# A vision-transformer kernel with its feed-forward, triangular solve and second attention in one unrolled phase, and the images solved in two groups

## The chip, the cores and the metric

The kernel runs on one core of one Trainium2 chip. The metric is the device time of one execution in microseconds (us), median over several runs. TensorE (PE) multiplies matrices into PSUM, VectorE (DVE), ScalarE (ACT) and GpSimd (POOL) work elementwise, and SyncE (SP) issues most transfers. GpSimd does not touch PSUM here. Engines run their own instruction streams in order and meet at semaphores.

## The reference, cut to what matters

64 images of 96x96 become 37 tokens of 256 features each. Then come: a first attention (16 query heads, one key/value head), a gated feed-forward whose gates are an entmax over 16 experts, a second attention that is a delta rule inside one chunk per image, and a mixture of 8 experts with one expert per token. The change lies in the feed-forward and the second attention, which for each image and each of two heads of 128 features is:

```python
k = x / max(norm(x), 1e-12)                    # x: the layernormed tokens, one head
beta = sigmoid(x @ W_beta.T); v = (x @ W_write.T) * beta; k_beta = k * beta
A0 = tril(-(k_beta @ k.T) * L, -1)             # L: decay by distance
A = solve_triangular(eye - A0, eye, lower=True, unit_diagonal=True)
v = A @ v                                      # state is zero: one chunk only
o = tril((k @ k.T) * L) @ v
h = h + layernorm(h) + o @ W_read.T            # roughly: the layer adds its own input
```

The solve is therefore 128 systems (64 images by 2 heads) of size 37x37.

## The kernel before, in words

Everything is fp32. 2368 token rows lie in SBUF as 22 tiles of 111 rows (3 images), worked on as 11 pairs of tiles. A phase is a block of the five engines' streams, ended by a barrier that also clears the phase's semaphores. The phases are:

1. Embedding and first attention, unrolled by hand. SyncE loads the first image tile, then the embedding weights (`in_params`), then the second tile; ScalarE's queue loads the identity and the other first weights, and, once `in_params` is there, 4.1 MB of later weights (lines 311 to 313 and 608 to 612). TensorE's first instruction waits for `in_params`.
2. Gates for all tiles at once, mostly on VectorE.
3. Feed-forward and keys (from line 880), a loop over pairs (`run_turns`, a hardware loop with a software pipeline three pairs deep). Per pair TensorE does `first_products`, `hidden` (eight chunks, through Gelu on ScalarE in `activate`), `second_products` (line 955), `outputs`, and, two turns later for each tile j, `turn_rows_and_keys` (line 979) and `row_products` (989, 995). VectorE does `gate_first`, `gate_second` (1092, each after a copy of the gate out of PSUM), `add_outputs` (1101), `normalise` (241 to 253), `key_squares`, `key_inverses` (1131, 1134) and `decay_products` (1141 to 1146). GpSimd does `prepare_keys` (250, 1175 to 1179). The normalised keys are a second set of rows, so a tile is transposed in four pieces: two of rows, two of keys.
4. The solve (from line 1184), for all 128 systems at once, one on each partition. VectorE scales the matrices by beta, SyncE stores them to `n_rows` in DRAM (line 1220) and loads them back with one system on a partition (1224), VectorE does the forward substitution (lines 1266 and 1272: one multiply and one reduce per row i = 1..36, in two column parts from i = 8 on, so that less is multiplied by zero), and SyncE stores the inverses to `a_rows` (1231). Behind the loads SyncE starts the 12.6 MB of expert weights that fit by now (1226, 1228).
5. Second attention (from line 1282), again `run_turns`. SyncE loads each tile's inverses (1304). Per tile: `spread_inverses` on GpSimd (1332), `solve_values` (1364), `attend` (1375), `read_out` (1386), `turn_rows` (1397) and `router_logits` (1407) on TensorE, copies on ScalarE, `add_and_norm` (1483, 241 to 253) and `keep_logits` (1495) on VectorE, and a store of the finished rows to `x_rows` (1311).
6. Routing (VectorE) and, at the end, 26 tiles of 128 gathered tokens through the experts (from line 1640). The change does not touch these.

Of the kernel before, what the change touches and what calls it, by code (L numbers as in the profile page):

```python
# [9 lines left out]

# [5 lines left out]
ALU = mybir.AluOpType  # L16
# [27 lines left out]
RL = 112  # L44
ROW_CUTS = ((0, 96), (96, R))
# [23 lines left out]
def build(nc, x_h, pack1_h, pack2_h, packc_h, w1_h, w2_h, out_h):  # L69
# [9 lines left out]
    with ExitStack() as top:  # L79
# [58 lines left out]
        beta_img = carve_1(NT * H1 * IPT, R)  # L138
        carve_1b = carver(arena_w2, W2S // 2)
        gate_t = carver(arena_w2, W2S // 2 + NT * H1 * R)(NT * R, E0)  # L140
# [3 lines left out]

        in_params = sem("in_params")
# [112 lines left out]
        with phase():  # L258
# [49 lines left out]
            @block.sync  # L308
            def _(sp):
                embed_w = at1["w_q"][0]  # L310
                sp.dma_start(xp[0], x_h[0]).then_inc(x_in[0], 16)
                sp.dma_start(pack1[:, 0:embed_w], pack1_h[:, 0:embed_w]).then_inc(in_params, 16)
                sp.dma_start(xp[1], x_h[1]).then_inc(x_in[1], 16)
                for i in range(1, PAIRS):
                    for j in range(2):
                        sp.wait_ge(embedded[j], i)
                        sp.dma_start(xp[j], x_h[2 * i + j]).then_inc(x_in[j], 16)

            @block.tensor
            def _(pe):  # L320
                pe.wait_ge(in_params, 16)
# [7 lines left out]
                def embed(i, j):  # L329
# [4 lines left out]
                    for k in range(PC):  # L334
                        mm = nc.tensor.matmul(bank[0][0:R, j * D:(j + 1) * D], xp[j][:, k * R:(k + 1) * R], w_lin[:, k, :],  # L335
# [270 lines left out]
            def _(act):  # L606
                embed_w = at1["w_q"][0]
                act.dma_start(ident, packc_h[:, 0:128]).then_inc(in_ident, 16)
                act.dma_start(pack1[:, embed_w:], pack1_h[:, embed_w:]).then_inc(in_qkv, 16)
                act.wait_ge(in_params, 16)  # L610
                for part, source, arrived in ((pack2, pack2_h, in_params2), (cst[:, 128:], packc_h[:, 128:], in_cst)):
                    act.dma_start(part, source).then_inc(arrived, 16)
                act.wait_ge(in_qkv, 16)
# [128 lines left out]
        with phase():  # L742
# [15 lines left out]
            beta = ec(NT * H1, R)  # L758
            nk = ec(NT * H1 * TOK, R)
# [112 lines left out]
        with phase():  # L872
            (z1_done, g1_out, z1_gated, hid_done, hid_act, z2_done, g2_out, z2_gated, y_done, y_added) = (
                psem(n) for n in ("z1_done", "g1_out", "z1_gated", "hid_done", "hid_act", "z2_done", "g2_out", "z2_gated",
                                  "y_done", "y_added"))
            stats = [pair("st"), pair("ag"), pair("ve")]
            (powered, normed, sq_done, roots, rooted, floored, inverted, k_ready, turned, t_ready, v_done, g_done,
             v_out, n_masked, n_reduced) = (
                pair(n) for n in ("powered", "normed", "sq_done", "roots", "rooted", "floored", "inverted", "k_ready",
                                  "turned", "t_ready", "v_done", "g_done", "v_out", "n_masked", "n_reduced"))  # L880
            rows_free = pair("rows_free")
            W = 2 * R
            bc = carver(arena_w1, n1w + n2w + 2 * H1 * R + 2 * H1 + NT * H1 * (TOK + 1))
            z1, z2, g1, g2 = (bc(W) for _ in range(4))
            hid = bc(OC * W)
            wc = carver(work)
            xn = [wc(D, R) for _ in range(2)]
            st = [wc(8, R) for _ in range(2)]
            ve = [wc(4, R) for _ in range(2)]
            cc = carver(arena_w1)  # L890
            kn = [cc(D, R) for _ in range(2)]
            xk = [cc(4 * R) for _ in range(2)]
            sq = [cc(D, R) for _ in range(2)]
            nf = [cc(H1 * R, R) for _ in range(2)]
            sc = [cc(12, R) for _ in range(2)]
            block = enter(nc.Block())


            HB = OC // 2
# [3 lines left out]

# [1009 lines left out]
```

## Time and profile before

| | |
|---|---|
| median of 3 runs | 863.99 us (863.92 to 864.47) |
| profiled execution | 865.1 us, of which the span on the page is 863.3 us |
| PE busy, share of span | 678.2 us (79%) |
| DVE busy | 455.9 us (53%) |
| ACT, POOL busy | 237.3 us (27%), 246.7 us (29%) |
| mean granted TensorE clock | 0.884 of full speed |

A share is a mean over phases that are bound by different engines, so the stages have to be read one by one. The profiled execution is 1.1 us above the median of the runs. Busy time of TensorE is modelled at its ends, and a matmul of fp32 shows as several records.

### The profile page before, as it was taken

What the parts mean: (1) busy time and instruction counts of PE and PEld (TensorE: products, weight loads), DVE (VectorE), ACT (ScalarE), POOL (GpSimd) and SP (SyncE); (2) the same over time, 40 slices, a digit from 0 to 9 for tenths busy, and PEclk for the clock granted to TensorE, in tenths of its full rate; (3) what the DMA queues carried; (4) which work ended last, traced back from release to release, by engine and by line L of the source; (5) the groups of instructions that cost most, each with busy time, mean ns of one, the idle gap of its engine ahead of it and who ended that gap; (6) DMA issues with size and microseconds to landing.
All of it is one profiled execution on the core that took longest, in us unless ns stands there. A gap on an engine that the chain in (4) does not pass through costs nothing. (4 is left out here: it accounts for less than half of the span.)

```text
span 863.3 us, 14177 instructions
## 1 busy us (share of the span) xinstructions
PE 678.2 (79%) x4606; PEld 513.0 (59%) x4606; DVE 455.9 (53%) x1216; ACT 237.3 (27%) x615; POOL 246.7 (29%) x330
## 2 busy tenths in 40 slices
PE   4799999999976079999994000899269999999995
PEld 2567777777754058888873000688156766776673
DVE  1457777777764826666765197366623333333331
ACT  0223333333321143424333000355103223323321
POOL 1344444444441003343342000233011122222211
PEclk9899999999986569999997555799659999999998
DMA  8111111111000000000000993322510111111110
GB/s 339 44 34 33 33 34 33 33 34 33 1 2 1 0 2 0 1 0 0 0 0 0 118 438 127 68 84 84 226 49 25 49 56 49 45 55 55 44 37 18
DMA packets 21542, 49.31 MB, mean 57 GB/s; under 512 B 12451, under 2 KB 12581, under 8 KB 20719
## 3 DMA queue, kind: packets, MB, share of 16 engines
q1 hardware_dynamic: 17583, 33.21, 12.8%
q0 software_dynamic: 3328, 10.23, 3.8%
q10 hardware_dynamic: 576, 5.15, 1.5%
q8 instruction: 33, 0.54, 0.2%
q14 instruction: 22, 0.18, 0.1%
HBM read 38.72 MB, written 9.86 MB: 56 GB/s over the span
## 5 line engine op out<-in xcount | busy, mean ns | idle before, releaser
L1707 PE MATMUL psum<-arena_w,work 128*128 x208 | 95.5, 603 | 1.0 <-DVE work L1759 1.0
L1805 ACT ACTIVATE work<-psum,cst 128x128 f32<-128x128 f32 x208 | 56.7, 383 | 144.0 <-PE psum L1720 143.9
L1731 PE MATMUL psum<-arena_w,work 128*128 x416 | 94.2, 379 | 0.4 <-ACT work L1805 0.4
L1731 PEld LDWEIGHTS psum<-arena_w,work 128*128 128x128 f32 x416 | 77.1, 190 | 10.5 <-issue 1.1
L1364 PE MATMUL psum<-tokens,work 111*111 (+1 forms) x88 | 16.1, 310 | 72.7 <-POOL work L1332 71.8
L1768 DVE COPY work<-psum 128x512 f32<-128x512 f32 x52 | 35.9, 691 | 69.8 <-PE psum L1707 69.8
L1669 POOL DMA_INDIRECT out<-work,row_i x26 | 25.7, 988 | 159.9 <-DVE work L1781 159.9
L335 PE MATMUL psum<-arena_w 128*111 128x256 f32 x264 | 64.2, 396 | 8.9 <-DMA arena_w<-in_pack 8.9
L1707 PEld LDWEIGHTS psum<-arena_w,work 128*128 128x128 f32 x208 | 38.2, 194 | 39.8 <-issue 39.8
L335 PEld LDWEIGHTS psum<-arena_w 128*111 128x111 f32 x264 | 46.8, 183 | 23.5 <-DMA arena_w<-in_pack 8.9
L704 POOL TENSOR_TENSOR arena_w<-arena_w,work 101x592 f32<-101x592 f32 x33 | 39.5, 1197 | 71.8 <-DVE work L566 71.8
L250 POOL TENSOR_TENSOR work<-work 111x1 f32<-111x1 f32 x44 | 24.4, 555 | 119.3 <-DVE work L246 119.3
L1364 PEld LDWEIGHTS psum<-tokens,work 111*111 111x111 f32 x88 | 12.0, 193 | 73.7 <-POOL work L1332 71.9
L695 POOL TENSOR_TENSOR arena_w<-arena_w 128x296 f32<-128x296 f32 x66 | 43.8, 685 | 22.3 <-DVE arena_w L534 22.3
L1775 DVE TENSOR_TENSOR tokens<-psum,cst 128x256 f32<-128x256 f32 x26 | 11.0, 424 | 73.6 <-PE psum L1731 73.6
L389 PE MATMUL psum<-arena_w 128*37 128x296 f32 x264 | 41.5, 436 | 3.3 <-ACT arena_w L658 3.3
L941 PE MATMUL psum<-arena_w 128*128 128x222 f32 x176 | 39.8, 372 | 1.7 <-DVE arena_w L1081 1.0
L627 ACT COPY arena_w<-psum 37x592 f32<-37x592 f32 x33 | 25.2, 765 | 57.7 <-PE psum L400 57.7
L546 DVE TENSOR_REDUCE work<-psum 101x16 f32<-101x592 f32 x33 | 25.4, 771 | 24.2 <-PE psum L389 24.2
L253 DVE TENSOR_SCALAR work<-tokens,work 111x256 f32 (+1 forms) x44 | 22.5, 512 | 29.5 <-POOL work L250 29.5
L941 PEld LDWEIGHTS psum<-arena_w 128*128 128x128 f32 x176 | 33.1, 198 | 7.3 <-issue 3.0
L955 PE MATMUL psum<-arena_w 128*128 128x222 f32 x176 | 36.2, 357 | 0.0
(214 smaller groups left out, 1332.8 us busy)
## 6 DMA issues: line engine op xcount, KB each, us to landing
arena_w<-in_w SPq DMA_DIRECT2D x2, 4096.0 KB, 13.8
arena_w<-in_x SPq DMA_DIRECT2D x22, 333.0 KB, 2.9
x_rows<-tokens SPq DMA_DIRECT2D x22, 192.0 KB, 2.0
arena_w<-in_pack ACTq DMA_DIRECT2D x1, 2420.0 KB, 8.5
cst<-in_packc ACTq DMA_DIRECT2D x1, 1727.0 KB, 13.1
arena_w<-in_pack SPq DMA_DIRECT2D x1, 1024.0 KB, 7.6
arena_w<-in_pack ACTq DMA_DIRECT2D x1, 818.5 KB, 8.1
work<-a_rows SPq DMA_DIRECT2D x22, 32.4 KB, 2.0
```

What stands on the lines that cost most here:

```text
L335: mm = nc.tensor.matmul(bank[0][0:R, j * D:(j + 1) * D], xp[j][:, k * R:(k + 1) * R], w_lin[:, k, :], start=(k == 0), stop=(k == PC - 1))
L389: mm = nc.tensor.matmul(bank[4 + f][e * HP:e * HP + TOK, 0:HH * TOK], qt[:, a:a + TOK], kb[p % 2 * 2 + e], start=True, stop=True)
L695: nc.gpsimd.tensor_tensor(kb[p % 2 * 2 + e].rearrange("p (h s) -> p h s", h=HH), kt[:, a:a + TOK].unsqueeze(1).broadcast_to([128, HH, TOK] ...
L704: nc.gpsimd.tensor_tensor(by_head(prob[p % 2], HP), by_head(prob[p % 2], HP), small[p % 2][:, 2 * NH:3 * NH].unsqueeze(2).broadcast_to([PR ...
L941: mm = nc.tensor.matmul(bank[2 + f // 2 % 2][:, (f % 2) * W:(f % 2 + 1) * W], w_out1[:, f, :], z1, start=True, stop=True)
L955: mm = nc.tensor.matmul(bank[1][:, W:2 * W], w_in2[:, f, :], hid[:, f * W:(f + 1) * W], start=(f == 0), stop=(f == OC - 1))
L1364: mm = nc.tensor.matmul(bank[j][0:R, h * 128:(h + 1) * 128], ab[j][:, h * R:(h + 1) * R], tokens[0:R, bass.ds((2 * i + j) * RW + D + h * 1 ...
L1669: pool.indirect_dma_start(out_h, bass.IndirectOffsetOnAxis(ap=row_i[:, 2 * i + j:2 * i + j + 1], axis=0), yo[j], None).then_inc(y_stored[j ...
L1707: mm = nc.tensor.matmul(bank[2 * j + f][:, :], xgt[j][:, k * 128:(k + 1) * 128], arena_w1[:, bass.ds(expert * (2 * FF) + (k * FF + f * 512 ...
L1731: mm = nc.tensor.matmul(bank[7][:, 0:D], ht[j][:, g * 128:(g + 1) * 128], arena_w2[:, bass.ds(expert * (FC * D) + g * D, D)], start=(g == ...
L1768: nc.vector.tensor_copy(hp[j][:, f * 512:(f + 1) * 512], bank[2 * j + f][:, :]).then_inc(h_out[j], 1)
L1805: nc.scalar.activation(ht[j][:, g * 128:(g + 1) * 128], bank[4 + f][:, k * 128:(k + 1) * 128], ACT.Gelu, bias=cst[:, bass.ds(expert * FC + ...
```

## The change

- The first transfers all go through SyncE's queue, in order of need, with the embedding weights in two halves; TensorE waits only for the half that it is about to use. The 4.1 MB of later weights start after the first attention's weights are there.
- Phases 3, 4 and 5 become one phase, unrolled in Python, without barriers in between.
- Keys are no longer normalised rows. The inverse norm of a head (`inv_all`) is folded into `beta`, into the strength that scales the system matrix, and into `add_read`. ScalarE makes the squares with a running sum (`squares`), beta comes from a Tanh in place of a Sigmoid over all tiles at the end, and GpSimd makes the small factors (`inverses`, `strengths`), which VectorE's scaling of the system matrices uses at once. Transposes per pair fall from 8 to 4.
- The two gate products are copied out of PSUM by ScalarE in one piece (`copy_gates`), not by VectorE in two. The reduction of the masked products over the three images is two adds on GpSimd (`fold`), and each tile's systems are stored as soon as they are made.
- The images are solved in two groups: pairs 0 to 5 (36 images, 72 systems) and pairs 6 to 10 (28 images, 56 systems). In the second group each system lies on two partitions, with every other column on each. VectorE takes the substitution in pieces between its other work: `SLOTS` gives the budget of each piece.
- SyncE's order: systems of group 0 stored, then loaded; systems of group 1 stored; inverses of group 0 stored; systems of group 1 loaded; inverses of group 0 loaded; 8.4 MB of expert weights; inverses of group 1 stored and loaded; 4.2 MB of expert weights; all finished rows.

The diff, cut to its core:

```diff
+GROUPS = ((0, 6), (6, PAIRS))
+SLOTS = (1.0, 1.0, 5.0, 1.7)
...
-                sp.dma_start(pack1[:, 0:embed_w], pack1_h[:, 0:embed_w]).then_inc(in_params, 16)
+                for k in range(2):
+                    part = slice(k * w_lin_w // 2, (k + 1) * w_lin_w // 2)
+                    sp.dma_start(pack1[:, part], pack1_h[:, part]).then_inc(in_embed[k], 16)
                 sp.dma_start(xp[1], x_h[1]).then_inc(x_in[1], 16)
+                sp.dma_start(pack1[:, w_lin_w:embed_w], pack1_h[:, w_lin_w:embed_w]).then_inc(in_params, 16)
+                sp.dma_start(ident, packc_h[:, 0:128]).then_inc(in_ident, 16)
+                sp.dma_start(pack1[:, embed_w:], pack1_h[:, embed_w:]).then_inc(in_qkv, 16)
...
-                pe.wait_ge(in_params, 16)
...
+                        if i == j == 0 and k % 3 == 0:
+                            pe.wait_ge(in_embed[k // 3], 16)
...
+                def load_systems(g):
+                    im0, im1, nb, stride, sets = group_of(g)
...
+                        sp.wait_ge(n_stored[b], 16 * len(ROW_CUTS) * len(range(b, stored, NB)))
...
+                for g in range(len(GROUPS)):
+                    for t in range(2 * GROUPS[g][0], 2 * GROUPS[g][1]):
+                        store_systems(t)
+                    if g:
+                        store_inverses(g - 1)
+                    load_systems(g)
+                for g in range(LAST):
+                    load_inverses(g)
...
+                sp.dma_start(arena_w1[:, :], w1_h).then_inc(w1_in, 16)
+                store_inverses(LAST)
+                load_inverses(LAST)
+                sp.dma_start(arena_w2[:, 0:W2S // 2], w2_h[:, 0:W2S // 2]).then_inc(w2a_in, 16)
+                for t in range(NT):
+                    sp.wait_ge(normed2, t + 1)
...
+                for i in range(-1, PAIRS + 2):
+                    second_products(i - 1)
+                    first_products(i)
+                    row_products(i - 2, 0)
+                    outputs(i - 1)
+                    hidden(i, range(OC // 2))
+                    row_products(i - 2, 1)
+                    gates(i + 1)
+                    hidden(i, range(OC // 2, OC))
+                    turn_rows(i - 1)
...
+                for t in range(NT + 3):
+                    solve_values(t)
+                    read_out(t - 1)
+                    turn_outputs(t - 3)
+                    attend(t)
+                    router_logits(t - 3)
...
+                    for k in range(2 * H1):
+                        a = 2 * H1 * i + k
+                        last = nc.scalar.activation(junk[:, k * 128:(k + 1) * 128], xn[i % 2][:, k * 128:(k + 1) * 128], ACT.Square,
+                                                    accum_out=ss[:, a:a + 1])
...
+                    nc.scalar.activation(th[:, t * H1:(t + 1) * H1], bank[6][0:R, D:D + H1], ACT.Tanh,
+                                         scale=0.5).then_inc(beta_out, 1)
+                    nc.scalar.copy(x_half(t), bank[6][0:R, 0:D]).then_inc(v_out, 1)
...
+                for i in range(-1, PAIRS + 2):
+                    copy_rows(i - 2)
+                    keep_values(i - 2, 0)
+                    activate(i, range(HB // 2))
+                    keep_values(i - 2, 1)
+                    copy_gates(i + 1)
+                    activate(i, range(HB // 2, HB))
+                    squares(i - 1)
...
+                    nc.vector.tensor_tensor(attn_t[:, t * H1 * R:(t + 1) * H1 * R], bank[7][0:R, 0:H1 * R], lt, ALU.mult)
+                    dve.wait_ge(strong, t + 1)
+                    free(dve, nk_ready, t - 1)
+                    for h in range(H1):
+                        cols = slice(h * R, (h + 1) * R)
+                        last = nc.vector.scalar_tensor_tensor(nf[t % 2][:, cols], bank[7][0:R, cols],
+                                                              strength[:, t * H1 + h:t * H1 + h + 1], ln[:, cols],
+                                                              ALU.mult, ALU.mult)
...
+                    nc.vector.memset(sys_x[:, 0:cols * TOK], 0.0).then_inc(zeroed[g], 1)
...
+                    dve.wait_ge(n_in[g], 16 * H1 * sets)
...
+                    yield 1.5
+                    last_cut = 0
+                    for i in range(1, TOK):
+                        cut = CUTS[i] // sets if CUTS[i] < i else i
...
+                            cost += 2 * (0.16 + (c1 - c0) * (end - j0) / 960)
...
+                def advance(budget):
+
+                    while pending[0] is not None and budget > 0:
+                        cost = next(pending[0], None)
+                        if cost is None:
+                            pending[0] = None
+                        else:
+                            budget -= cost
...
+                    for k, mark in enumerate((half_added, added)):
+                        nc.vector.scalar_tensor_tensor(h, bank[4 + j][0:R, k * D:(k + 1) * D],
+                                                       inv_all[:, t * H1 + k:t * H1 + k + 1], h,
+                                                       ALU.mult, ALU.add).then_inc(mark, 1)
...
+                for i in range(-1, PAIRS + 2):
+                    gate_second(i - 1)
+                    gate_first(i)
+                    advance(SLOTS[0])
+                    if i - 2 in ends:
+                        advance(math.inf)
+                    decay_products(i - 2, 0)
+                    add_outputs(i - 1)
+                    advance(SLOTS[1])
+                    normalise(i - 1)
+                    decay_products(i - 2, 1)
+                    if i - 2 not in ends:
+                        advance(SLOTS[2])
+                    elif ends[i - 2] < LAST:
+                        pending[0] = substitution(ends[i - 2])
+                advance(math.inf)
+                pending[0] = substitution(LAST)
+                firsts = [2 * p0 for p0, _ in GROUPS]
+                for t in range(NT + 3):
+                    if t == firsts[LAST]:
+                        advance(math.inf)
+                    normalise_outputs(t - 2)
+                    add_read(t - 1)
+                    keep_logits(t - 3)
+                    if t > 0:
+                        advance(SLOTS[3])
...
+                for i in range(-1, PAIRS + 2):
+                    strengths(i - 2, 0)
+                    fold(i - 2, 0)
+                    power_rows(i - 1)
+                    strengths(i - 2, 1)
+                    add_rows(i - 1)
+                    fold(i - 2, 1)
+                    inverses(i - 1)
+                for t in range(-1, NT + 1):
+                    power_outputs(t - 1)
+                    spread_inverses(t + 1)
```

## Rows read from the trace of the kernel before

**Rows 1.** The page's part 2: TensorE's busy tenths and granted clock in 40 slices.

```profile
PE   4799999999976079999994000899269999999995
...
PEclk9899999999986569999997555799659999999998
```

**Rows 2.** Stretches: length; busy PE, PEld, DVE, ACT, POOL; PE clock; DMA share; GB/s.

```profile
342.74:355.22 12.48, 12.48 (x70) 11.05 (x69) 8.36 (x25) 5.14 (x14) 4.72 (x8) 1.00 0.01 2
...
446.27:472.50 26.23, 15.37 (x69) 11.89 (x68) 14.35 (x41) 7.90 (x24) 9.02 (x14) 0.80 0.00 0
472.50:495.40 22.90, 0.00 (x0) 0.00 (x0) 3.50 (x6) 0.22 (x1) 0.41 (x1) 0.50 0.84 95
495.40:533.20 37.80, 0.00 (x0) 0.00 (x0) 36.74 (x130) 0.00 (x0) 0.00 (x0) 0.50 0.73 313
...
542.40:551.50 9.10, 8.07 (x32) 7.01 (x33) 1.99 (x6) 1.81 (x5) 2.68 (x5) 0.54 0.47 67
551.50:603.70 52.20, 50.57 (x345) 42.60 (x343) 34.46 (x115) 27.29 (x78) 19.99 (x37) 1.00 0.29 84
603.70:610.30 6.60, 4.02 (x24) 3.03 (x23) 3.03 (x13) 2.15 (x7) 1.10 (x2) 0.88 0.35 102
```

**Rows 3.** Timeline of TensorE in the feed-forward: start, duration, engine, line.

```profile
330.26 3.29 PE L955 MATMUL psum<-arena_w 128*128 128x222 f32 x16
...
338.92 0.35 PE L979 MATMUL psum<-cst,work 111*128 111x111 f32 x2
...
339.11 0.35 PE L979 MATMUL psum<-cst,arena_w 111*128 111x111 f32 x2
...
406.99 3.29 PE L955 MATMUL psum<-arena_w 128*128 128x222 f32 x16
```

**Rows 4.** Groups of instructions of VectorE and ScalarE by shape, 350 to 630 us.

```profile
L241 DVE BATCH_NORM_STATS2 work<-tokens 111x6 f32 x31 | 13.3, 428 | 4.6 <-issue 2.2
...
L1141 DVE TENSOR_TENSOR arena_w<-psum,arena_w 111x222 f32 x15 | 5.8, 390 | 0.0
L1101 DVE TENSOR_TENSOR tokens<-tokens,psum 111x512 f32 x8 | 5.4, 679 | 0.0
...
L1092 DVE SCALAR_TENSOR_TENSOR arena_w<-psum,arena_w 128x222 f32<-128x222 f32 x8 | 3.6, 451 | 0.3
...
L1065 ACT ACT_TABLE_LOAD x1 | 1.3, 1283 | 0.1
```

**Rows 5.** Timeline around the solve and into the second attention, all engines.

```profile
475.01 6.95 SPq L1220 DMA_DIRECT2D n_rows<-arena_w  x4
...
489.22 1.15 SPq L1224 DMA_DIRECT2D arena_w<-n_rows  x2
...
539.00 12.02 SPq L1304 DMA_DIRECT2D work<-a_rows  x22
...
542.36 1.08 POOL L1332 TENSOR_TENSOR work<-work,arena_w 111x222 f32<-111x222 f32 x2 [68.24 <-DMA work<-a_rows]
...
548.42 0.42 DVE L1483 TENSOR_TENSOR tokens<-tokens,psum 111x256 f32<-111x256 f32 x1 [9.25 <-PE psum L1386]
...
576.44 0.69 PE L1364 MATMUL psum<-tokens,work 111*111 x4
```

**Rows 6.** DMA issues of the page's part 6: KB each, median us to landing.

```profile
a_rows<-arena_w SPq DMA_DIRECT2D x2, 342.2 KB, 4.0
x_rows<-tokens SPq DMA_DIRECT2D x22, 30.0 KB, 2.0
```

**Rows 7.** The first transfers and matmuls: stretches of the span, then the timeline.

```profile
0.00:10.00 10.00, 1.14 (x3) 0.91 (x4) 1.46 (x5) 0.00 (x0) 2.85 (x9) 1.00 0.82 289
...
8.86 8.35 PE L335 MATMUL psum<-arena_w 128*111 128x256 f32 x24 [8.86 <-DMA arena_w<-in_pack]
```

**Rows 8.** Two lines of VectorE: duration in ns, least, median, most.

```profile
L253 DVE TENSOR_SCALAR work<-tokens,work x44: 412/414/644, 328.5 to 607.7; 111x256 f32 x32, 111x256 f32<-111x256 f32 x12
...
L1131 DVE TENSOR_SCALAR arena_w<-arena_w x22: 158/678/684, 330.9 to 465.3; 111x2 f32<-111x2 f32 x22
```

More of the change, by code:

```diff
@@ L872, in build @@
         with phase():
[L873 to L880, printed above, removed]
@@ new lines, in build @@
+            n_in, solved, a_stored, zeroed, diagonal = (
+                [psem(f"{name}{g}") for g in range(len(GROUPS))]
+                for name in ("n_in", "solved", "a_stored", "zeroed", "diagonal"))
+            chain = pair("chain")
+            a_in = [psem(f"a_in{t}") for t in range(NT)]
+            x_stored = psem("x_stored")
+            block = enter(nc.Block())
+            W = 2 * R
+            HB = OC // 2
+            LAST = len(GROUPS) - 1
+            fc = carver(arena_w1, n1w + n2w + 2 * H1 * R + 2 * H1)
@@ L1010, in _, with solve_values @@
-                run_turns(pe, turn, behind=2)
+                        key = xk[:, (2 * j + h) * R:(2 * j + h + 1) * R]
+                        mm = nc.tensor.matmul(bank[7][0:R, h * R:(h + 1) * R], key, key, start=True, stop=True)
+                    mm.then_inc(g_done, 1)
+                def solve_values(t):
+                    if not tile(t):
+                        return
+                    pe.wait_ge(a_block, t + 1)
+                    free(pe, vn_out, t - 1)
+                    for h in range(H1):
+                        mm = nc.tensor.matmul(bank[t % 2][0:R, h * 128:(h + 1) * 128], ab[t % 2][:, h * R:(h + 1) * R],
+                                              x_half(t)[:, h * 128:(h + 1) * 128], start=True, stop=True)
+                    mm.then_inc(vn_done, 1)
@@ new lines, in attend @@
+                def attend(t):
+                    if not tile(t):
+                        return
+                    pe.wait_ge(vn_out, t + 1)
+                    free(pe, o_out, t - 1)
+                    for h in range(H1):
+                        a = (t * H1 + h) * R
+                        mm = nc.tensor.matmul(bank[2 + t % 2][:, h * R:(h + 1) * R], vn[t % 2][:, h * 128:(h + 1) * 128],
+                                              attn_t[:, a:a + R], start=True, stop=True)
+                    mm.then_inc(o_done, 1)
@@ new lines, in router_logits @@
+                def router_logits(t):
+                    if not tile(t):
+                        return
+                    pe.wait_ge(xt_ready, t + 1)
+                    for k in range(2):
+                        mm = nc.tensor.matmul(bank[6 + t % 2][0:R, 2 * R:2 * R + NE], xt[t % 2][:, k * R:(k + 1) * R],
+                                              w_r[:, k, :], start=(k == 0), stop=(k == 1))
+                    mm.then_inc(logits, 1)
+                for i in range(-1, PAIRS + 2):
[8 more added lines that the diff above has]
+                    turn_rows(i - 1)
```

884 lines of the change are left out of this document (399 added, 485 removed).

## The prediction

> **What bounds the kernel now.** I read first TensorE's busy tenths and clock over the span [rows 1]. TensorE is full except in three places: a gap near 280 to 310 us (gates), one from about 455 to 545 us, and routing near 615 us. The change works on the second, and on the first microseconds.
>
> The busy times by stretch [rows 2] show what the second gap is made of. A steady turn of the feed-forward lasts 12.48 us with TensorE busy for all of it and VectorE for 8.36. From 446.27 the pipeline runs out for 26.2 us. Then 22.9 us pass with every engine nearly idle (systems to DRAM and back), 37.8 us with VectorE alone (the solve), and 9.2 us, up to the start of the row at 542.40, of storing and reloading inverses. TensorE does nothing for 69.9 us. In the second attention it is busy again for 50.57 of 52.2 us, so that stage is bound by TensorE at 2.7 us a tile.
>
> The largest possible gain is thus some 70 us. The question is how much of the solve finds room on VectorE. The mistake to avoid is to count it as hidden because two stages overlap: solving is VectorE's work, and VectorE has work of its own in both.
>
> **The start.** The first matmul starts at 8.86 us, when all 1 MB of embedding weights has landed, together with 1.2 MB of others; 289 GB/s flowed meanwhile [rows 7]. It now needs the first tile and half the weights, 0.73 MB: 2.5 us at that rate, plus 0.8 us to the first issue and about 2 us for a transfer to land [rows 6]. I take 4.9 us, so 4 us gained; TensorE has 8.35 us of embedding right behind it, in which the other parts land. Bounds: nothing (the same landing) and 5.5 us (bytes only). The later weights start a little later and nobody waits for them.
>
> **Feed-forward, turns 1 to 7.** TensorE bounds them. Two groups of transposes start 0.19 us apart and the whole four of a tile take 0.54 us [rows 3]; four of eight go, so a turn is 12.48 - 0.55 = 11.93 us. The removed gate copies, key squares and inverses lay on VectorE and GpSimd beside it: worth nothing here, but they make the room for the solve. The first turn gets a second gate product, a copy and some waiting: +1.3. The old turns 2 to 7 took 406.99 - 330.26 = 76.7 us [rows 3], a little over 12.48 each. New turn 8 starts at 330.26 + 1.4 + 6 x 11.93 = 403.2 against 406.99.
>
> **Turns 8 to 12, with group 0's solve.** From here VectorE is the chain. Its own work in a turn [rows 4]: two gatings at 0.45, four times 0.30 (half as wide as 0.45's) and two times 0.39 for the masked products, 0.68 to add, two times 0.43 and three short ones at 0.16 (as two elements take at least in line 1131 [rows 8]) for the statistics, two times 0.41 (line 253) to normalise; with waits 6.2 us. Fewer partitions do not shorten an instruction, so group 0 costs what all the systems cost: 37.8 us [rows 2], and 1.2 for the clearing. The step costs in the code say which steps fall where: 12 steps in turn 8 (6.9 us with the clearing), 8 in turn 9 (6.3), 6 in turn 10 (7.3), 5 in turn 11 (7.9), and the last 5, the largest, in turn 12 before its masked products (10.5). VectorE also meets the wait for the loaded systems at the start of turn 8, in front of everything else: two small stores and a load after the last fold, against 4.7 us before the piece is reached. I take 2.7 us lost. The chain is 3.2 (until the second products) + 3 x 6.2 + 5.7 + 2.7 (turns 11 and 12, which have no new pair) + 39 + 2.7 = 71.9. Feed-forward ends at 475.1, and a fold on GpSimd makes it 476. Before it was 472.5 [rows 2]. So hiding group 0 gives nothing yet; it only moves work of the solve into a stage that grows by what it had gained.
>
> **Into the second attention.** SyncE then issues in order: the last stores, inverses of group 0, a wait of 2 us for landing [rows 6], four loads of systems, the loads of inverses. At some 0.5 us each the first inverses are asked for at 482, and as before it is 3.4 us to GpSimd and 0.6 (one of the two spreadings) to TensorE [rows 5]: 485.1 and 485.7. That is 9.7 us of idling where there were 70.
>
> **First 12 tiles, with group 1's solve.** VectorE's first addition came 6.1 us after GpSimd's first spreading [rows 5], so now at 491.2. Own work per tile: two additions at 0.45, statistics 0.43 and three short ones, 0.41 to normalise, 0.16 for the logits; with the gaps of a chain 2.75 us. Group 1 is spread over two partitions each, so it multiplies 6653 elements instead of 12472, but the 130 instructions remain, each with its fixed part: 27.9 us, and 0.9 for the clearing, against 37.8. VectorE needs 2.0 + 10 x 2.75 + 28.8 = 58.3, hence 549.5. TensorE alone would need 33. Its clock is low after the idling [rows 2], at 1.2 GHz a tile costs it about 4.9 us (an estimate: twice the 2.6 us that it is busy per tile, less some fixed parts) against VectorE's 4.4, so I add 1.5: solved at 551. The last 11 us of that come in one piece before tile 12, with TensorE idle.
>
> **Last 10 tiles.** The inverses of group 1 leave in 2072 pieces of 148 bytes. The 4884 such pieces of line 1220 took from 475.0 to 489.2 [rows 5], so 6 us, and 2 to land; bounds 4.0 (large pieces [rows 6]) and 11. Then 4.0 to TensorE: 563. From tile 12 to the end it took 610.3 - 576.44 = 33.9 us [rows 2, 5]. It is 4.5 more because the clock is down again at the start (9 us at half speed, as at 542 to 551 [rows 2]), and 1 because VectorE's 2.75 is now just above TensorE's 2.7: 602.4. I leave the finished rows and the 4.2 MB of weights beside it at nothing: they have 40 us. If they were late, the barrier at the end would wait.
>
> **GpSimd beside the solve.** Before, GpSimd was idle in the solve; now it works beside it. Line 253 takes 412 ns, and 644 where GpSimd works at the same time; line 1131, with two elements, takes 678 instead of 158 [rows 8]. No row shows a multiplication of two SBUF operands there. Bounds: nothing, and 15 us (below). Nearest in kind is the solve's own stream, which shows nothing: I take 2. The Trainium skill (GPSIMD Engine Reference, Key points) says that GpSimd contends with VectorE instructions that run in a two-port mode or have two SBUF inputs; the multiplications are of that second sort. By it the sum would lie near the upper bound; that is a rival below.
>
> **Sum**, against the trace of before: second attention ends at 602.4 + 2 instead of 610.3, that is -5.9, and -4 at the start: -9.9. The profiled execution took 865.1, 1.1 above the median, so I take the difference from the median: 863.99 - 9.9 = 854.1, say 854.
>
> **Rivals.**
> First, the pieces fit better: VectorE's gaps of 0.4 to 0.9 us a turn vanish behind solve instructions, the store of small pieces takes 4 us, the clock stays high. That is 2 + 4 + 4 us: 844. For it speaks that interleaved chains fill each other's waits; against it that TensorE idles twice for some 10 us or more.
> Second, the ends slip: VectorE's waits (loaded systems in turn 8, strengths from GpSimd) and the late rows at the end cost 2 us at some four places: 861.
> Third, and on the other side: each multiplication sits out a running GpSimd instruction, as line 1131 does. GpSimd will be busy for about half of a feed-forward turn, so 33 of group 0's 65 multiplications meet one, and lose 0.35 us on average; in the attention a quarter of 65 lose 0.25. That is 15 us in place of 2: 867, slower. It decides from a mean loss of 0.1 us per multiplication. The rule of the Trainium skill cited above (GPSIMD Engine Reference, Key points) is this rival. From the rows, for it speaks that line 1131 does wait like that [rows 8], against it that both lines there are of another kind.
> Fourth, table loads: one costs 1.28 us [rows 4], and if Tanh and Gelu do not share a table, four fall into each turn, two of them between a hidden product and its Gelu. ScalarE's 6.2 us of a turn become 11.3, with waits the turn becomes 14: 11 x 2 = 22 us, 876. No row shows Tanh. The Trainium skill (ScalarE: Activation LUTs, Table sets) lists tanh with exp and with sigmoid and not with gelu; by it these loads would come.
>
> **Chances.** Forecast 0.50, first rival 0.20, second 0.14, third 0.11, fourth 0.05. A measurement can tell 0.2%, or 1.7 us. Faster: the first three less a tail of the second, 0.82; within 0.2%: 0.03; slower 0.15. The range leaves out the fourth, part of the third and a tail below the first: 841 to 866.
>
> **What would show it.** First matmul near 5 us; turns of 11.9 us up to the eighth and of 12 to 15 after it with VectorE full; TensorE idle for about 10 us near 480 and for 20 or more near 545 to 563; about 4.4 us a tile before that and 2.7 after; last logits some 6 us before 610 plus the start's 4. It would be wrong if the solve's multiplications are longer than before at the same width, if ScalarE shows more than one table load in the phase, or if one of the two idle stretches is missing.

## The result, and the profile after

The changed kernel takes 876.4 us (median of 4 runs, 870.6 to 880.5) against 864.2 for the kernel before on the same chip: a ratio of 1.013, interval 1.007 to 1.019. It is slower by 1.3%. The forecast was 854, with 841 to 866 as its range. The profiled execution took 880.5, the slowest of the four, with a span of 878.7 and a mean granted clock of 0.852; the fastest had 0.875.

TensorE's busy tenths and clock of the kernel after, which answer to [rows 1]:

```profile
PE   5899999999963299999833774377459999999994
...
PEclk8899999999975579999965556556559999999998
```

The gap of zeros is gone, as the change promised. In its place stand ten slices (some 220 us, from about 440 to 660) in which TensorE is busy for three to seven tenths of the time at five to six tenths of its clock. The last two of them are routing, where the kernel before is as low. Its second attention (slices 26 to 28) starts with an eight and a seven and has nines in both lines after that.

Stretches of the kernel after, columns as in [rows 2]: the feed-forward from turn 8 on, then the first twelve tiles of the second attention and the last ten, each from the first start to the last.

```profile
400.00:412.00 12.00, 12.00 (x68) 10.98 (x67) 10.27 (x44) 5.14 (x18) 5.83 (x16) 1.00 0.13 36
...
424.00:436.00 12.00, 11.03 (x61) 9.87 (x60) 11.93 (x41) 4.61 (x17) 6.56 (x16) 1.00 0.04 8
436.00:448.00 12.00, 5.67 (x26) 3.97 (x25) 11.93 (x36) 2.56 (x13) 6.30 (x16) 0.83 0.02 3
448.00:460.00 12.00, 3.26 (x11) 2.17 (x9) 12.00 (x24) 0.87 (x4) 2.01 (x5) 0.64 0.02 3
...
473.41:535.67 62.26, 43.94 (x177) 37.40 (x177) 36.44 (x156) 10.62 (x30) 12.42 (x21) 0.61 0.34 138
561.61:614.27 52.66, 39.41 (x163) 33.57 (x163) 22.03 (x63) 9.54 (x27) 9.68 (x18) 0.59 0.48 166
```

The first four rows go as forecast: VectorE fills up with the solve of the first group. The last two do not. In the last, nine tiles in 52.66 us are 5.85 us a tile, with no solve beside them (VectorE busy for 22 of 52.7 us), where the kernel before had 2.7 [rows 2]. No engine is full. Where no engine is full, a ring of waits is to be looked for, and the timeline shows it whole; these are all the links between the products of tile 13 and those of tile 14:

```profile
567.63 1.19 PE L1130 MATMUL psum<-tokens,work 111*111 111x128 f32 x4 [1.32 <-POOL work L1537]
...
568.62 1.91 PE L1151 MATMUL psum<-cst,work 128*111 128x256 f32 x4
...
570.57 1.00 DVE L1417 SCALAR_TENSOR_TENSOR tokens<-psum,arena_w,tokens 111x256 f32<-111x256 f32 x2 [2.84 <-PE psum L1151]
...
571.61 0.43 DVE L1421 BATCH_NORM_STATS2 work<-tokens 111x6 f32<-111x256 f32 x1
...
572.07 0.18 DVE L1423 BATCH_NORM_AGGREGATE work<-work 111x2 f32<-111x6 f32 x1
572.28 0.15 DVE L1425 TENSOR_SCALAR work<-work 111x1 f32<-111x1 f32 x1
...
572.52 0.55 POOL L1547 TENSOR_TENSOR work<-work 111x1 f32<-111x1 f32 x1 [4.94 <-DVE work L1425]
573.03 0.56 POOL L1537 TENSOR_TENSOR work<-work,arena_w 111x222 f32<-111x222 f32 x1
...
573.64 1.19 PE L1130 MATMUL psum<-tokens,work 111*111 111x128 f32 x4 [1.32 <-POOL work L1537]
```

Read it as a chain. Products of tile 13 (line 1130) at 567.63, behind them in TensorE's order the read-out of tile 12 (1151), on VectorE its additions (1417) and statistics (1421 to 1425), on GpSimd its power (1547), and behind that in GpSimd's order the block of tile 14 (1537, the spread of the inverses), for which the products of tile 14 wait. One turn of the ring is 6.01 us. TensorE's wait is put down to line 1537; but that instruction took 0.56 us and its inputs were there long before. It stood behind the power in GpSimd's queue. In the kernel before, GpSimd spread tile t + 1 before it took the power of tile t - 1.

### The profile page after: what moved, and what is told of

The parts are those of the page before. It is cut to its first block and busy times, and to the rows that moved or that the text cites. A ratio compares the mean times of both kernels' runs of the same rounds, so it can differ in the third digit from the quotient of the medians.

```text
span 878.7 us, 13690 instructions
## 1 busy us (share of the span) xinstructions
PE 702.9 (80%) x4562; PEld 540.4 (62%) x4562; DVE 450.1 (51%) x1266; ACT 228.7 (26%) x635; POOL 260.0 (30%) x418
## 5 line engine op out<-in xcount | busy, mean ns | idle before, releaser
L1786 PEld LDWEIGHTS psum<-arena_w,work 128*128 128x128 f32 x416 | 77.1, 190 | 10.5 <-issue 1.1
L1130 PE MATMUL psum<-tokens,work 111*111 111x128 f32 x88 | 23.2, 410 | 64.1 <-POOL work L1537 64.1
L1417 DVE SCALAR_TENSOR_TENSOR tokens<-psum,arena_w,tokens 111x256 f32<-111x256 f32 x44 | 21.3, 484 | 71.9 <-PE psum L1151 71.1
L1130 PEld LDWEIGHTS psum<-tokens,work 111*111 111x111 f32 x88 | 16.9, 264 | 66.4 <-POOL work L1537 54.9
L702 POOL TENSOR_TENSOR arena_w<-arena_w 128x296 f32<-128x296 f32 x66 | 43.9, 687 | 20.7 <-DVE arena_w L545 20.7
L1547 POOL TENSOR_TENSOR work<-work 111x1 f32<-111x1 f32 x22 | 13.2, 601 | 104.1 <-DVE work L1425 104.1
L1069 PE MATMUL psum<-arena_w 128*128 128x222 f32 x176 | 40.9, 379 | 0.5 <-DVE arena_w L1283 0.5
L1151 PE MATMUL psum<-cst,work 128*111 128x256 f32 x88 | 39.9, 605 | 0.0
```

The costliest lines, as they stand in the source:

```text
L702: nc.gpsimd.tensor_tensor(kb[p % 2 * 2 + e].rearrange("p (h s) -> p h s", h=HH), kt[:, a:a + TOK].unsqueeze(1).broadcast_to([128, HH, TOK] ...
L1069: mm = nc.tensor.matmul(bank[2 + f // 2 % 2][:, (f % 2) * W:(f % 2 + 1) * W], w_out1[:, f, :], z1, start=True, stop=True)
L1130: mm = nc.tensor.matmul(bank[t % 2][0:R, h * 128:(h + 1) * 128], ab[t % 2][:, h * R:(h + 1) * R], x_half(t)[:, h * 128:(h + 1) * 128], sta ...
L1151: mm = nc.tensor.matmul(bank[4 + t % 2][0:R, h * D:(h + 1) * D], ot[t % 2][:, h * R:(h + 1) * R], w_read[:, h, :], start=True, stop=True)
L1786: mm = nc.tensor.matmul(bank[7][:, 0:D], ht[j][:, g * 128:(g + 1) * 128], arena_w2[:, bass.ds(expert * (FC * D) + g * D, D)], start=(g == ...
```

## The experiments

Theory A is this ring: GpSimd's new order is the cause. Rivals were: B, TensorE's low clock alone; C, VectorE's two additions per tile in place of one.

**1. GpSimd's order turned round in the changed kernel.**

```diff
 for t in range(-1, NT + 1):
-    power_outputs(t - 1)
     spread_inverses(t + 1)
+    power_outputs(t - 1)
```

> The changed kernel, with GpSimd's two instructions of a tile in the second attention exchanged: the spreading of the inverses for tile t + 1 is issued before the power for the statistics of tile t - 1, not behind it. Theory A (a loop through GpSimd's order: products of tile t, read-out of t - 1, VectorE's additions and statistics, power, spreading, products of t + 1) expects the steps of 6.0 us between tiles to fall to about 2.75 us in the last ten tiles and to 4.4 to 4.9 us in the first twelve, where VectorE's solve then bounds: 843 us in all. Theory B (TensorE is slow because its clock stays at 1.2 GHz after two idle stretches, whatever the order) expects 5 us a tile and more to remain, and 865 to 880 us. Theory C (the doubled additions make VectorE the bound) expects no change, 876 us.

835.5 us (833.8 to 836.7), ratio to the kernel before 0.966 (0.963 to 0.969). Two lines, the same work, 41 us. That is the cause of the loss, and it leaves the rest of the change as a gain of 29 us, where 10 had been forecast. The time is below theory A's 843 although the pace is not: from the fifth of the last ten tiles on they came every 3.085 us and not every 2.75, with TensorE waiting 0.35 us for GpSimd each time. Experiments 6 to 8 look into that.

**2. The converse: GpSimd's spread put late in the kernel before.**

```diff
-                    spread_inverses(following, 0)
+                    spread_inverses(this, 1)
...
-                    spread_inverses(following, 1)
+                    spread_inverses(following, 0)
```

Behind the power of tile s GpSimd now spreads tile s + 2, as in the changed kernel, and no longer s + 3.

> The kernel before, with only GpSimd's order in the second attention made as in the changed kernel: each spreading one place later, behind the power of the tile before the last. Theory A expects a tile to take 4.0 us at the full clock and 5.4 us at half of it instead of 2.7 us, with TensorE waiting for the spreading at every tile: 892 us (full clock throughout) to 922 us (half throughout). Theories B and C expect 864 us, since neither the idle stretches nor VectorE's work is changed.

917.6 us (two runs, 917.3 and 917.9), ratio 1.061 (1.057 to 1.065). The late spread, in a kernel with none of the change, costs 53 us. The tiles came 5.8 us apart, or 4.7 to 5.1 where the clock was high for a part of the tile, instead of 2.7. Its trace has the same order as the one above, the spread (line 1332) behind the power (line 250) and TensorE waiting for it:

```profile
600.71 0.55 POOL L250 TENSOR_TENSOR work<-work 111x1 f32<-111x1 f32 x1 [4.01 <-DVE work L246]
...
601.23 0.56 POOL L1332 TENSOR_TENSOR work<-work,arena_w 111x222 f32<-111x222 f32 x1
...
601.95 1.19 PE L1364 MATMUL psum<-tokens,work 111*111 x4 [1.11 <-POOL work L1332]
```

**3. Is the clock cause or consequence? Three matmuls more per tile.** They fill TensorE's wait, and change no order.

```diff
 for t in range(NT + 3):
+    for _ in range(3 if 1 < t < NT else 0):
+        nc.tensor.matmul(bank[t % 2][:, 256:512], ident, w_read[:, 0, :], start=True, stop=True)
     solve_values(t)
```

> The changed kernel with three matmuls more at the start of each tile of the second attention (tiles 2 to 21; 128x128 by 128x256, into a bank that the tile's first products overwrite), nothing else touched: they fill TensorE's wait for GpSimd. If the lower clock (0.60 in these stretches) is a consequence of the wait and makes it longer, the granted clock should rise to 0.9 or more; then products (1.19 to 0.69 us) and read-out (1.91 to 1.03) shorten the ring of 6.02 us to 4.7, to which the three matmuls (0.4 us each at the full clock) add up to 0.4 where they end after the block is there: 4.7 to 5.1 us a tile, 22 x 1.1 = 24 us less, 848 to 858 us, in spite of more work. If the clock plays no part in the pace, 876; if it stays low, the added matmuls (0.8 us each) end after GpSimd's block and the time goes up, to 885 or 900.

859.7 us (858.1 to 860.8), ratio 0.993 (0.990 to 0.995): 17 us less than the changed kernel, by added work, and just above the expected 848 to 858. The granted clock was 0.92 in the first twelve tiles and 0.96 in the last ten (1.00 from the second of these on), where the changed kernel had 0.61 and 0.59. The last tiles in its trace (a stretch of one tile, then the timeline):

```profile
561.50:566.18 4.68, 4.14 (x24) 3.27 (x25) 2.45 (x8) 1.06 (x3) 1.07 (x2) 1.00 0.84 264
```

```profile
561.50 0.69 PE L1130 MATMUL psum<-tokens,work 111*111 111x128 f32 x4 [0.54 <-POOL work L1539]
...
563.10 1.00 DVE L1419 SCALAR_TENSOR_TENSOR tokens<-psum,arena_w,tokens 111x256 f32<-111x256 f32 x2 [1.50 <-PE psum L1151]
...
566.18 0.69 PE L1130 MATMUL psum<-tokens,work 111*111 111x128 f32 x4 [0.54 <-POOL work L1539]
```

From the products to the additions it is 1.60 us at the full clock (561.50 to 563.10) and 2.94 at half of it (567.63 to 570.57 above). The difference, 1.34, is the whole difference between 6.02 and 4.68 us a tile. So the ring is the cause and the clock its amplifier: the wait leaves TensorE idle for part of each tile, the granted clock falls, and the matmuls that lie in the ring take longer. The saving is less than 22 x 1.34 = 29 us, since the changed kernel had some tiles at the high clock and its first half other waits. B alone is refuted: at the full clock a tile still takes 4.68 us and the kernel 24 us more than in experiment 1. But some 17 of the 41 us are the clock's.

**4. One addition left out of the changed kernel.** It leaves out the first head's half of the read-out: the loop keeps k = 1. (The expectation below names the second; the two halves are of the same size and lie in the same place of the ring.)

```diff
-for k, mark in enumerate((half_added, added)):
+for k, mark in ((1, added),):
```

> The changed kernel with only the first of the two additions of the read-out on VectorE (484 ns each): it leaves out the second head's half of each tile's read-out. Theory A (the additions lie in the ring): 6.02 - 0.50 = 5.5 us a tile, 22 x 0.5 = 11 us less, 865.5 us, from 863 to 868 with the clock. Rival (VectorE is off the chain here, busy 37.6 of 60 us): under 1 us, 875 to 877.

860.0 us (856.0 to 866.0, 9 runs), ratio 0.993 (0.990 to 0.997). That is 16 us less than the changed kernel, more than theory A's 11, and the trace shows why (products of tiles 12 to 15):

```profile
548.78 1.20 PE L1130 MATMUL psum<-tokens,work 111*111 111x128 f32 x4 [21.74 <-POOL work L1537]
...
554.28 1.20 PE L1130 MATMUL psum<-tokens,work 111*111 111x128 f32 x4 [0.80 <-POOL work L1537]
...
559.78 0.69 PE L1130 MATMUL psum<-tokens,work 111*111 111x128 f32 x4 [0.98 <-POOL work L1537]
...
563.93 0.69 PE L1130 MATMUL psum<-tokens,work 111*111 111x128 f32 x4 [1.42 <-POOL work L1537]
```

A tile takes 5.50 us at the low clock, 0.5 less than the changed kernel's 6.02, and 4.15 to 4.2 at the high one, 0.5 less than experiment 3's 4.68. A shorter ring leaves TensorE busy for a larger share, so more of the tiles are at the high clock: the granted clock of the last ten tiles was 0.73, for 0.59. C is right in so far as the additions lie in the ring; as the cause it is refuted by experiment 1, which keeps both.

**5. One group, on top of experiment 1.**

```diff
-GROUPS = ((0, 6), (6, PAIRS))
+GROUPS = ((0, PAIRS),)
```

> As e1_spread_first, and all 64 images solved in one group between feed-forward and second attention, so nothing of the solve is hidden (the phase stays unrolled, without barriers, with systems stored per tile). If hiding in two groups is worth what it costs, this is slower than e1_spread_first, by up to 30 us. My reckoning says the opposite: feed-forward ends 12 us sooner, the solve takes 38 us alone, then 22 tiles run at 2.75 us: 831 us, some 12 us below e1_spread_first.

831.6 us (831.0 to 832.8), ratio 0.961 (0.958 to 0.964): with the solve in one piece and nothing hidden, 4 us less than with two groups. The last masked product ends at 448.3 instead of 463.2, the inverses leave at 494.64, the first tile starts at 502.2, and from the fourth tile on it is again 3.085 us a tile. That the 831 of the expectation was met is in part luck: it had 2.75 us a tile, and 843 for experiment 1, and was 12 us below that, not 4.

**6. A third block buffer, so that GpSimd spreads one tile further ahead.**

```diff
-ab = [wc(H1 * R, R) for _ in range(2)]
+ab = [wc(H1 * R, R) for _ in range(3)]
...
-for t in range(-1, NT + 1):
-    spread_inverses(t + 1)
+for t in range(-2, NT + 1):
+    spread_inverses(t + 2)
```

> One group and GpSimd's spread ahead of its power, as in the experiment with one group (831.6 us), and one tile more of lead: a third block buffer, so that GpSimd writes the block of tile t + 2 before it takes the power of tile t - 1. Theory A (a ring through GpSimd): the ring products 1.2, copies, read-out 1.0, additions and statistics 1.8, power 0.55, spread 0.56 is about 6.0 us long and closes over one tile in the changed kernel (6.02 us a tile), over two with the spread first (3.085 us a tile, TensorE 0.35 us idle at each for GpSimd); over three it would be 2.0 us a tile, so TensorE's own work decides: 2.7 us a tile, no wait for GpSimd, 22 x 0.37 = 8 us less, about 823.5 us. Rival: the 3.085 us are TensorE's own pace or VectorE's, and the 0.35 us only sit beside them: 831, within 1.

830.3 us (829.5 to 831.0), ratio 0.959 (0.956 to 0.962): 1 us, where theory A had 8: a miss. The rival's number came out (831, within 1), but not its reason, which was TensorE's or VectorE's own pace, as experiments 7 and 8 will show. TensorE's wait for GpSimd was gone, and from the seventh tile on the pace was the old one. In its trace the wait had moved to the transposes:

```profile
523.06 0.67 PE L1130 MATMUL psum<-tokens,work 111*111 111x128 f32 x4
...
524.88 0.41 PE L1161 MATMUL psum<-cst,tokens 111*128 111x111 f32 x2 [0.29 <-DVE tokens L1432]
...
526.13 0.67 PE L1130 MATMUL psum<-tokens,work 111*111 111x128 f32 x4
```

A wait that moves when its releaser is taken away was a symptom. The timeline of experiment 5 (one group, two blocks) has the ring that holds both:

```profile
526.18 0.69 PE L1130 MATMUL psum<-tokens,work 111*111 111x128 f32 x4 [0.34 <-POOL work L1537]
526.20 0.99 DVE L1417 SCALAR_TENSOR_TENSOR tokens<-psum,arena_w,tokens 111x256 f32<-111x256 f32 x2
...
528.13 0.55 POOL L1547 TENSOR_TENSOR work<-work 111x1 f32<-111x1 f32 x1 [2.01 <-DVE work L1425]
...
528.65 0.56 POOL L1537 TENSOR_TENSOR work<-work,arena_w 111x222 f32<-111x222 f32 x1
528.72 0.64 DVE L1432 TENSOR_SCALAR tokens<-tokens,work 111x256 f32<-111x256 f32 x1 [0.59 <-POOL work L1547]
...
529.28 0.99 DVE L1417 SCALAR_TENSOR_TENSOR tokens<-psum,arena_w,tokens 111x256 f32<-111x256 f32 x2
```

VectorE adds and takes the statistics of a tile (526.20 to 528.13), waits 0.59 us for GpSimd's power, normalises that tile (line 1432), and only behind that, in its own order, come the additions of the next: 1.93 + 0.59 + 0.56 = 3.08 us. Theory D: this second ring sets the 3.085.

**7 and 8. VectorE's order turned round too,** with three blocks (on experiment 6) and with two (on experiment 5).

```diff
-normalise_outputs(t - 2)
 add_read(t - 1)
+normalise_outputs(t - 2)
```

> The third block buffer took GpSimd's wait away from TensorE's first products (none left in its trace) and the pace stayed at 3.085 us a tile. In that trace VectorE waits 0.59 us a tile for GpSimd's power before it normalises tile t - 2, and the additions of tile t - 1 stand behind that: additions 0.99, statistics 0.43 + 0.18 + 0.15, power 0.55 with its hand-over, normalisation 0.64, about 3.08 us. Theory D (a second ring, VectorE to GpSimd's power and back, of the same length as the first): with the additions of tile t - 1 put ahead of the normalisation of tile t - 2 in VectorE's order, and three blocks, VectorE has only its own 2.55 us and TensorE its own 2.7: 2.7 to 2.8 us a tile, 20 x 0.33 = 6.6 us less than 830.3, 823.7 (822 to 826). Rival: 3.085 us are what TensorE takes at this clock (its work 3.0 us a tile with weight loads): 830, within 1.

> One group, GpSimd's spread first, two block buffers, and VectorE's additions ahead of its normalisation. Theory D: the second ring is gone, the first one, through GpSimd's spread over two tiles, stays: 6.0 / 2 = 3.0 us a tile, 20 x 0.08 = 1.6 us less than 831.6: 830 (829 to 831), with TensorE's waits for GpSimd's spread still there. If it comes to 824 too, the ring through the spread was never a limit by itself; if it stays at 3.085, VectorE's order isn't one.

With three blocks 821.3 us (820.1 to 822.3), ratio 0.949 (0.947 to 0.952); with two 819.8 us (817.9 to 822.3), ratio 0.947 (0.944 to 0.950). Theory D holds: both are 9 to 12 us faster than without the swap. The 829 to 831 expected with two blocks were missed, so the third block is worth nothing: I had divided the 6.0 us of the first ring by two tiles, but those are at half clock; at the full clock it is 4.68, so 2.34 a tile, below TensorE's own 2.573. A stretch and the timeline with two blocks:

```profile
515.00:550.00 35.00, 35.00 (x248) 29.90 (x247) 29.05 (x96) 14.49 (x42) 15.28 (x26) 1.00 0.52 174
```

```profile
531.23 0.67 PE L1130 MATMUL psum<-tokens,work 111*111 111x128 f32 x4
...
532.02 0.41 DVE L1432 TENSOR_SCALAR tokens<-tokens,work 111x256 f32<-111x256 f32 x1
...
532.19 0.65 POOL L1547 TENSOR_TENSOR work<-work 111x1 f32<-111x1 f32 x1 [1.40 <-DVE work L1425]
...
533.81 0.67 PE L1130 MATMUL psum<-tokens,work 111*111 111x128 f32 x4
```

TensorE is busy for 35.00 of 35 us. This is the version that beats both kernels, by some 46 us (the one before, by the ratio) and 57 (the changed one, by the medians).

**9. Two groups again, with both orders mended.** The diff to the changed kernel is that of experiment 1 and that of 7.

> The changed kernel with two groups kept, GpSimd's spread ahead of its power, and VectorE's additions ahead of its normalisation. The second half of the attention goes from 3.085 to 2.573 us a tile as with one group, 10 x 0.51 = 5 us less than 835.5; in the first half VectorE waits no longer for the power (0.59 us a tile) but has the second group's solve between, so that up to 12 x 0.5 = 6 us more: 828 (823 to 831). That two groups cost more than they hide: it stays above the 819.8 of one group by 4 us (835.5 - 831.6) or more. Rival: with the rings gone two groups hide what they were meant to: below 819.

832.5 us (831.1 to 834.1), ratio 0.963 (0.959 to 0.967), somewhat above the range. The rival is refuted: two groups cost 12.7 us against one. And VectorE's order, worth 12 us with one group, is worth 3 here (835.5 to 832.5). The first tile starts 30.9 us earlier (470.61 for 501.53), yet tile 12 starts 4.9 later (538.69 for 533.81), after 24.6 us of TensorE idling, and the last nine intervals take 3.7 more, the first two of them at the low clock.

**10. VectorE's order alone, in the changed kernel** (the diff of 7 and nothing else).

> The changed kernel with VectorE's additions ahead of its normalisation and nothing else: GpSimd's power still stands ahead of its spread. The normalisation of tile t - 2 is not in the ring of 6.02 us (its power was taken a tile earlier), so nothing changes there: 876, between 873 and 878. Rival: VectorE's order alone was the fault (it gave 12 us where the spread came first): 12 us or more less, 864 or below.

877.2 us (875.3 to 879.1), ratio 1.014 (1.010 to 1.019): no change, as theory A has it. The second ring lies hidden under the first and is worth something only once that is gone: 3 us in this kernel with its two groups (experiments 1 and 9), 12 with one group (5 and 8).

**11. The first transfers alone, in the kernel before.** It is that part of the change; its core:

```diff
-sp.dma_start(pack1[:, 0:embed_w], pack1_h[:, 0:embed_w]).then_inc(in_params, 16)
+for k in range(2):
+    part = slice(k * w_lin_w // 2, (k + 1) * w_lin_w // 2)
+    sp.dma_start(pack1[:, part], pack1_h[:, part]).then_inc(in_embed[k], 16)
...
+sp.dma_start(pack1[:, w_lin_w:embed_w], pack1_h[:, w_lin_w:embed_w]).then_inc(in_params, 16)
+sp.dma_start(ident, packc_h[:, 0:128]).then_inc(in_ident, 16)
+sp.dma_start(pack1[:, embed_w:], pack1_h[:, embed_w:]).then_inc(in_qkv, 16)
...
-pe.wait_ge(in_params, 16)
...
+if i == j == 0 and k % 3 == 0:
+    pe.wait_ge(in_embed[k // 3], 16)
```

> The kernel before with the first transfers alone changed: one queue, in order of need, embedding weights in halves. The forecast's term: first matmul at 4.9 us instead of 8.86 and 4 us off the total, 860 us. If the gain is lost again behind the later weights, 864 us and a second pair of tiles that starts no earlier.

858.5 us (857.8 to 859.5), ratio 0.992 (0.990 to 0.995), some 6 us less. The first matmul starts at 4.79 instead of 8.86, which gives 4.1; 1.4 more is in the first embedding, 6.99 us long for 8.35 [rows 7]:

```profile
4.79 6.99 PE L342 MATMUL psum<-arena_w 128*111 128x256 f32 x24 [4.79 <-DMA arena_w<-in_pack]
```

In the changed kernel, with the same start, that row has 8.26. Why the two differ wasn't tried.

## Why the prediction was wrong

The rows of the changed kernel for the steps, timeline view: first matmul; the steady turns; leaving of the inverses (the queue of SyncE); first tile of either half.

```profile
4.76 8.26 PE L346 MATMUL psum<-arena_w 128*111 128x256 f32 x24 [4.76 <-DMA arena_w<-in_pack]
...
464.84 0.77 SPq L1000 DMA_DIRECT2D a_rows<-arena_w  x2
...
473.41 1.16 PE L1130 MATMUL psum<-tokens,work 111*111 111x128 f32 x4 [11.21 <-POOL work L1537]
...
551.88 2.01 SPq L1000 DMA_DIRECT2D a_rows<-arena_w  x4
...
561.61 1.19 PE L1130 MATMUL psum<-tokens,work 111*111 111x128 f32 x4 [21.79 <-POOL work L1537]
```

**The start**: forecast 4.9, measured 4.76. Right, with a little luck: the three parts named for it (2.5, 0.8 and 2) add up to 5.3.

**Feed-forward, turns 1 to 7**: forecast 11.93 us a turn, measured 11.70. Right, and 1.4 us better over the six turns that the sum multiplies.

**Turns 8 to 12**: the mechanism was right, VectorE is full from 412 on and TensorE falls to 3.3 of 12 us. The size was off: 71.9 us were forecast from turn 8 to the last masked product, and it was 66.3 (396.9 to 463.2). My 6.2 us of own work with waits per turn was too much: VectorE was idle for only 6.5 of the 66.3 us, so the solve's pieces fill most of the waits. So the first tile was on TensorE at 473.4; the forecast, less the 4 us of the start, has 481.7.

**Last 10 tiles, and First 12 tiles: the steps that failed.** They were put at 2.7 us a tile ("TensorE's 2.7") and 4.4 ("VectorE's 4.4"), each from the busiest engine. The trace has 6.0 or 5.2 for both kinds. In sum: tile 0 came 8.3 us early; from tile 0 to tile 12 it took 88.2 us instead of 77.3, 10.9 more, of which the second group's solve hid a part; and from tile 12 to the last logits 63.1 instead of the 39.4 of the sum, 23.7 more. That is 26.3 us, less the forecast's 2 for contention 24.3, of the 25.3 between the forecast for a profiled execution (865.1 - 9.9 = 855.2) and the 880.5 measured. The step had costed every instruction, and had not followed GpSimd's new order. GpSimd was busy for 20 of 52 us in that stage [rows 2], and its power and its spread cost the same in either order, so the swap looked free. A moved instruction has two prices, its duration and what now stands in front of it. None of my rivals had the second.

The ring is not the whole of the error, and without it the forecast would have been wrong on the other side. In experiment 1, where the ring is mended, tile 0 starts at 473.6 (8.1 us early), tile 12 follows after 66.8 us for 77.3, and the last logits 38.3 us later for 39.4. With the 2 for contention that is 21.7 us less than forecast. Most of the 10.5 us in the middle is the term for VectorE's own work and the second group's solve together: 57.4 us from tile 0 to the leaving of the inverses, for 65.3. So 854 lay 22 us below the changed kernel because some 41 us that it lacked stand against some 20 us that it had too much.

**Last piece of the solve, and the trip of the inverses**: the bubble was forecast (11 us of solve in one piece, then 12 of trip) and it is there, 21.8 us; the trip was 9.7 us (551.88 to 561.61) against 12: the loads were issued at 559.06, 7.2 after the stores for 8 forecast, and 2.5 more brought the first tile where 4.0 were forecast.

**GpSimd beside the solve, the third rival**: the solve's multiplications (line 1383) and its sums (1390) in the feed-forward, first group:

```profile
L1383 DVE TENSOR_TENSOR work<-arena_w 72x9 f32<-72x9 f32 (+19 forms) x65 | 22.2, 376 | 0.7
L1390 DVE TENSOR_REDUCE arena_w<-work 72x3 f32<-72x9 f32 (+19 forms) x65 | 19.9, 342 | 0.2
```

The 65 multiplications took 22.2 us for 20.7 in the kernel before, when GpSimd was idle; the sums, with one input, 19.9 for 20.3. In experiment 5, the same unrolled phase with GpSimd idle beside the solve, it is 20.7 and 20.3 again. So contention is there, 1.5 us of it (forecast 2), a mean of 23 ns where the rival needed 100. (The second group's multiplications have other widths, and nothing in the kernel before compares with them.) The rule of the Trainium skill (GPSIMD Engine Reference, Key points), that instructions with two SBUF inputs contend with GpSimd, agrees in kind.

**Table loads, the fourth rival**: one load of 1.28 us in the phase, with Gelu, Tanh, squares and copies in it. The rival gives nearly the measured time by another mechanism, so its number is no merit. The Trainium skill (ScalarE: Activation LUTs, Table sets) has tanh in other sets than gelu's; the trace disagrees, since no load stands between the two.

**What was not forecast either: two groups don't pay.** I had noted that "group 0 costs what all the systems cost" (now measured: 42.1 us for its 130 instructions, 41.0 for all the systems before). The whole solve is then 38 us of VectorE in one group and, by the forecast's own terms (37.8 + 28.8), some 67 in two. Hiding the first ended the feed-forward 14.9 us later (463.2 for 448.3), and the second left its largest steps over. Experiment 9 has the sum.

## What to carry to other kernels

Where work of one engine is put in another order, write down for each tile the ring that runs through that engine's queue: who waits for the last instruction, what stands before it, what that waits for, and over how many tiles the ring closes. The length by the number of tiles is a bound of its own, beside every engine's busy time. When no engine is full, look for it, and when mending one wait only moves it, look for the second ring, which may be as long as the first. Cutting work into groups to hide it pays only if a group costs less than the whole; instructions that don't get shorter with fewer partitions don't (here 42.1 us for 72 systems and 41.0 for 128).

## What the runs showed of the hardware

Added matmuls made the kernel faster: 17 us less with 60 of 128x128 by 128x256 more, and the granted clock went from 0.61 to 0.92 in the first twelve tiles of the attention and from 0.59 to 0.96 in the last ten.

VectorE's normalisation (one SBUF tensor as input, line 1432) takes 0.64 us where it starts beside GpSimd's spread of 0.56 us, and 0.41 where it doesn't (the fences of experiments 5 and 8; the medians of all 22 are 0.640 and 0.404). In experiment 8 it is GpSimd's power of one element that is longer, 0.65 for 0.55 us, where it starts while the normalisation runs. So the two lengthen each other, also in an instruction with one tensor input. That the later one waits for the earlier is the likely reading; no run separates it from both running slower.
